# Recurrence stage: rows turned by DMA transposes, three projections in float16 halves, some waits moved

## What is computed

```python
# bounded product (L0_ffn)
out = jnp.einsum('bln,nk->blk', x, weight) * scale
v_norm = jnp.maximum(jnp.linalg.norm(out, axis=-1, keepdims=True), EPS)
out = out * (jnp.tanh(v_norm) / (v_norm + EPS))
out = out * jnp.minimum(MAX_NORM_RATIO / jnp.maximum(norm(out), EPS), 1.0)
# recurrence (L1_attn)
y = jax.nn.gelu(jnp.einsum('btd,dl->btl', x, w_y) + b_y, approximate=False)
xb = jnp.einsum('btd,dl->btl', x, w_x) + b_x
conv = conv_b + sum(conv_w[k] * xp[:, k:k + Tn] for k in range(4))   # xp: xb, padded
gate_x = jax.nn.sigmoid(jnp.einsum('btl,lm->btm', conv, w_ig) + b_ig)
gate_a = jax.nn.sigmoid(jnp.einsum('btl,lm->btm', conv, w_ag) + b_ag)
a = jnp.exp(-8.0 * gate_a * jax.nn.softplus(a_param))
h = a * h + gate_x * conv * jnp.sqrt(1.0 - a * a)                      # over the tokens
out = jnp.einsum('btl,ld->btd', h * y, w_out) + b_out
```

## Time and profile before

| what | us |
|---|---|
| median of 3 runs (1032.4 to 1034.07) | 1033.49 |
| the profiled execution | 1033.6 |
| its span, first to last instruction | 1031.9 |
| PE busy | 999.0 (97%) |
| DVE busy | 810.9 (79%) |
| ACT busy | 648.2 (63%) |
| step 2 of the recurrence, by its window | 36 |

### The profile page before, as it was taken

How to read it: one execution, slowest core, us unless ns; L and a number is a source line. 1 busy time by engine, 2 the same in 40 slices (tenths; PEclk the granted TensorE clock), 3 DMA queues, 4 the chain that set the end, 5 groups by cost and what they waited for, 6 DMA issues and landing times. The chain is left out here.

```text
span 1031.9 us, 19678 instructions
## 1 busy us (share of the span) xinstructions
PE 999.0 (97%) x7402; PEld 832.3 (81%) x7402; DVE 810.9 (79%) x1429; ACT 648.2 (63%) x1339; POOL 335.0 (32%) x456
## 2 busy tenths in 40 slices
PE   6899999999999999999999999989999999999997
PEld 6789898999989887999999989975445875875873
DVE  5998999999999998876867776885858766766763
ACT  7968786867777685665566566666232761762750
POOL 2004334152414134425344443513421331331331
PEclk9999999999999999999999999999999999999999
DMA  7520313214040454501001102023601201101101
GB/s 231 205 99 33 131 63 99 104 58 149 13 156 6 139 173 166 215 1 42 19 27 42 43 1 84 32 101 102 225 1 63 61 2 63 62 2 51 32 1 62
DMA packets 44703, 81.38 MB, mean 79 GB/s; under 512 B 7360, under 2 KB 17600, under 8 KB 42560
## 3 DMA queue, kind: packets, MB, share of 16 engines
q1 hardware_dynamic: 44608, 80.11, 22.6%
HBM read 67.24 MB, written 12.85 MB: 78 GB/s over the span
## 5 line engine op out<-in xcount | busy, mean ns | idle before, releaser
L2311 PE MATMUL banks<-d_wd,d_hh 128*128 128x512 f16 x256 | 98.1, 383 | 2.1 <-DVE d_wd L2038 2.1
L2311 PE MATMUL banks<-d_wd,d_hl 128*128 128x512 f16 x256 | 98.0, 383 | 0.0
L650 DVE SCALAR_TENSOR_TENSOR a_xs<-a_xpre,a_cvec,a_xs 128x256 f32<-128x256 f32 x192 | 91.2, 543 | 0.4 <-ACT a_xs L453 0.4
L1887 POOL TENSOR_TENSOR d_hl<-d_h32s,d_hh 128x512 f16<-128x512 f32 x48 | 55.7, 1160 | 97.4 <-ACT d_hh L1982 97.4
L822 PE MATMUL banks<-a_xth,a_wgh 128*128 128x256 f32 x256 | 74.3, 290 | 1.7 <-DVE a_wgl L592 1.7
L675 DVE TENSOR_TENSOR_SCAN a_L<-a_L,a_ident 128x512 f32<-128x512 f32 x64 | 74.8, 1212 | 0.5
L822 PE MATMUL banks<-a_xth,a_wxh 128*128 128x256 f32 x256 | 74.6, 291 | 0.0
L822 PE MATMUL banks<-a_xtl,a_wxh 128*128 128x256 f32 x256 | 72.5, 283 | 0.0
L822 PE MATMUL banks<-a_xth,a_wxl 128*128 128x256 f32 x256 | 72.4, 283 | 0.0
L822 PE MATMUL banks<-a_xtl,a_wgh 128*128 128x256 f32 x256 | 72.2, 282 | 0.0
L822 PE MATMUL banks<-a_xth,a_wgl 128*128 128x256 f32 x256 | 72.2, 282 | 0.0
(11 more groups left out here) (361 smaller groups left out, 3338.9 us busy)
## 6 DMA issues: line engine op xcount, KB each, us to landing
a_L<-decays SPq DMA_DIRECT2D x16, 1024.0 KB, 4.8
a_xf<-in_x_turned SPq DMA_DIRECT2D x16, 256.0 KB, 3.8
a_xr<-in_x SPq DMA_DIRECT2D x16, 256.0 KB, 2.7
tokens<-a_xr SPq DMA_DIRECT2D x16, 256.0 KB, 2.0
c_xb<-tokens SPq DMA_DIRECT2D x16, 256.0 KB, 2.7
d_xin<-tokens SPq DMA_DIRECT2D x16, 256.0 KB, 4.2
d_r<-tokens SPq DMA_DIRECT2D x16, 256.0 KB, 2.7
d_wd_codes<-in_down_w SPq DMA_DIRECT2D x4, 1024.0 KB, 9.3
```

The costliest lines, as they stand in the source:

```text
L650: ins = dve.scalar_tensor_tensor(out=out, in0=xpre[:, m, k:k + T], scalar=cvec[:, m, k:k + 1], in1=out, op0=ALU.mult, op1=ALU.add)
L1887: pool.tensor_tensor(hl[:, m, :], (h32s[:, m % 4, :] if i else h32[:, m % 2, :]), hh[:, m, :], ALU.subtract).then_inc(s_hl, 1)
L2311: ins = pe.matmul(ps_o[:, c % 2, :], h[:, m, cols(c)], wd[:, m, :], start=(m == 0 and h is hh), stop=(m == M - 1 and h is hl), skip_group_ ...
```

## The change

1. **Float16 halves.** Bounded, x and y use float16 instead of float32r: rows times 1024 (`X_TOP`), each weight times a factor from its norm. The factor comes from sums of squares: those of the bounded weight are built in mixer steps 1 to 5 from four small loads (`wpart`) that SP issues, with a wait for the square of the one before; those of w_x and w_y by two big ACT squares in the mixer's last step (`weight_squares`). Five small products on PE (`weight_sum`), a clip on DVE and three POOL operations (`weight_scale`) make the factors of it. The inverse factors go into the scale of the gelu, of the x projection's copy, and into c_scl (`scale_in`).
2. **Rows of steps 2 to 7.** PE's `turn_in` stays for rows 0 and 1. For the others ACT writes the high half of the untransposed rows (`rows_h`), DVE the low half (`rows_l`), and SP issues eight DMA transposes for each half (`turn_rows`, sixteen a step, 128x128 float16), for which PE's `bounded` waits.
3. **Waits moved.** In step 0 PE waits for the mixer's mean squares after the first half of the x projection and after `turn_in(1)`. `output(6)` is split in two as `output(7)` was. DVE takes `scaled(s+1)` ahead of `low_hy(s-1)`; in step 6 two of four conversions go behind `squared`. In the feed-forward stage `product` goes ahead of two conversions, and `down(0, 0)` waits for d_wd pair by pair.

The diff, cut to its core:

```diff
@@ mamba2, sync @@
+                if s <= KD:
+                    sp.wait_ge(s_wsq, 64 + 17 * (s - 1))
+                    sp.dma_start(wpart, pieces[NW][0][:, s - 1, :]).then_inc(s_wsq, 16)
                 store(s - 1)
@@ mamba2, scalar @@
+            if n is None and m is not None:
+                act.wait_ge(s_norms, 3 if i == NW else 6)
+                act.activation(hi, staged(i), ACT.Copy, scale=m).then_inc(s_whi, 1)
...
+        def weight_squares(i):
+            act.wait_ge(s_stage[i % 4], 16 * (i // 4 + 1))
+            n = KD + i - NW - 1
+            act.activation(pieces[i][1], staged(i), ACT.Square, scale=1.0 / W_TOP, accum_out=wsq[:, n:n + 1]).then_inc(s_wsq, 1)
...
             else:
-                high_piece(NW + 1)
+                weight_squares(NW + 1)
+                weight_squares(NW + 2)
+                following_stage["scale_in"]()
             own_heads(C * s + 1)
...
             high_y(C * s)
+            if 2 <= s < KD + 2:
+                part_squares(s - 2)
...
         following_stage["softplus"](1)
+        high_piece(NW + 1)
         high_piece(NW + 2)
@@ bounded_rg_lru, tiles @@
-    xth = sb_early("c_xth", [P, KD, T], F32R)
+    xth = sb_early("c_xth", [P, KD, T], F16)
...
+    sb_rows = Sbuf(nc, room["raw_y"], room["raw_y"] + 8 * KD * T)
+    rows_h, rows_l = sb_rows("c_rowsh", [P, C, D], F16), sb_rows("c_rowsl", [P, C, D], F16)
...
+    def turned(s):
+        return 2 * C + max(0, s - 1) * 2 * C * KD * 16
@@ bounded_rg_lru, sync @@
+        def turn_rows(s):
+            for src, dst, made in ((rows_h, bxh, s_bh), (rows_l, bxl, s_bl)):
+                for j in range(C):
+                    sp.wait_ge(made, C * s + j + 1)
+                    for k in range(KD):
+                        sp.dma_start(dst[:, k, cols(j)], src[:, j, k * P:(k + 1) * P], transpose=True).then_inc(s_bt, 16)
...
             for s in range(NS - 2):
+                turn_rows(s + 2)
                 if s + SLOTS < NS:
@@ bounded_rg_lru, scalar @@
             for j in range(C):
+                if s >= 2:
+                    act.wait_ge(s_x[s % SLOTS][j], 16 * (s // SLOTS + 1))
+                    act.wait_ge(s_bt, turned(s - 1))
+                    act.activation(rows_h[:, j, :], slot(s)[:, j, :], ACT.Copy, scale=X_TOP).then_inc(s_bh, 1)
+                    continue
                 act.wait_ge(s_bt, C * s + j + 1)
-                act.activation(bxh[:, :, cols(j)], ps_t[:, j], ACT.Copy).then_inc(s_bh, 1)
+                act.activation(bxh[:, :, cols(j)], ps_t[:, j], ACT.Copy, scale=X_TOP).then_inc(s_bh, 1)
@@ bounded_rg_lru, vector @@
                 dve.wait_ge(s_bh, C * s + j + 1)
+                if s >= 2:
+                    dve.wait_ge(s_x[s % SLOTS][j], 16 * (s // SLOTS + 1))
+                    dve.scalar_tensor_tensor(out=rows_l[:, j, :], in0=slot(s)[:, j, :], scalar=X_TOP, in1=rows_h[:, j, :], op0=ALU.mult, op1=ALU.subtract).then_inc(s_bl, 1)
+                    continue
...
                     recur(s - 1)
+                    if s + 1 < NS:
+                        scaled(s + 1)
                     low_hy(s - 1)
...
-                    for i in range(4):
+                    for i in range(2):
                         following_stage["convert"](i)
@@ bounded_rg_lru, tensor @@
-                pe.wait_ge(s_bl, C * s + j + 1)
+                if s < 2:
+                    pe.wait_ge(s_bl, C * s + j + 1)
+                else:
+                    pe.wait_ge(s_bt, turned(s))
...
-            if s + 1 == NS:
+            if s + 2 >= NS:
                 pe.wait_ge(s_hyh, s + 1)
...
+        def after_sums(then):
+            then(1)
+            pe.wait_ge(*last["mean_sq"])
...
-                if s + 2 < NS:
-                    turn_in(s + 2)
@@ gated_ffn @@
                 if c == 0:
                     pe.wait_ge(s_hl, M * i + m + 1)
+                    if i == 0 and m % 2 == 0:
+                        pe.wait_ge(s_prep_down, m // 2 + 1)
...
-                    pe.wait_ge(s_prep_down, len(pieces) - M)
                     down(i, 0)
```

More of the change, by code:

```diff
@@ L21 @@
 EARLY = 7
+X_TOP = 1024.0
+W_TOP = 2.0 ** 14
+W_TINY = 1e-30
 class Sbuf:
@@ L210, in mamba2 @@
     NX, NG, NW = 5, 9, len(pieces)
-    for raw, src, hi, lo in following:
-        pieces.append((src, hi, lo, None, None))
+    for raw, src, hi, lo, of_weight in following:
+        pieces.append((src, hi, lo, None, of_weight))
     def staged(i):
@@ L588, in low_piece @@
         def low_piece(i):
-            _, hi, lo, _, m = pieces[i]
+            _, hi, lo, n, m = pieces[i]
             dve.wait_ge(s_whi, i + 1)
-            if m is None:
+            if n is None and m is not None:
+                dve.scalar_tensor_tensor(out=lo, in0=staged(i), scalar=m, in1=hi, op0=ALU.mult, op1=ALU.subtract).then_inc(s_wlo, 1)
+            elif m is None:
                 dve.tensor_tensor(lo, staged(i), hi.bitcast(F32), ALU.subtract).then_inc(s_wlo, 1)
@@ L887, in sum_sq, with weight_sum @@
             last.then_inc(s_sp, 1)
+            if n == C * (KD + 2) - 2:
+                weight_sum(True, slice(0, 1))
+        def weight_sum(first, own):
+            pe.wait_ge(s_wsq, squared - (2 if first else 0))
+            if not first:
+                pe.wait_ge(s_norms, 3)
+            for k in range(KD if first else 1):
+                src = wsq[:, k:k + 1] if first else wsq[:, KD:KD + 2]
+                last = pe.matmul(ps_n[not first], ones.broadcast_to([P, P]), src, start=k == 0, stop=k == KD - 1 or not first)
+            last.then_inc(s_norms, 1)
         def x_proj(s, p):
@@ L1018, in mamba2 @@
             "gate": (s_gate, 4 * NS), "output": (s_op, C * NS), "low_output": (s_yl, C * (NS - 1)),
-            "again": {**again, "small": Again(s_small, 64), "late": Again(s_L[0], 16 * NS), "down": Again(s_L[1], 16 * NS),
+            "again": {**again, "small": Again(s_small, squared), "late": Again(s_L[0], 16 * NS), "down": Again(s_L[1], 16 * NS),
                       "x": [Again(s_stage[i], 16 * len(range(i, len(pieces), 4))) for i in range(4)],
@@ L1508, in main @@
                 squared(s)
+                if s == NS - 2:
+                    for i in range(2, 4):
+                        following_stage["convert"](i)
                 if s == 1:
@@ L2179, in main @@
                 for m in range(early, M if i == 0 else 0):
+                    for op, j in {9: ((0, 0),), 11: ((1, 0), (0, 2)), 13: ((1, 2),), 14: ((0, 4),)}.get(m, ()):
+                        weight_sums(op, j)
+                    product(i, m)
                     if 7 <= m < 10:
@@ L2182, in main @@
                         convert(2 * m - 3)
-                    for op, j in {9: ((0, 0),), 11: ((1, 0), (0, 2)), 13: ((1, 2),), 14: ((0, 4),)}.get(m, ()):
-                        weight_sums(op, j)
-                    product(i, m)
                     if m >= 12:
```

89 lines of the change are left out of this document (64 added, 25 removed).

## The result

| | before | after |
|---|---|---|
| median, us | 1033.04 | 1151.72 (1150.71 to 1152.64) |
| ratio | | 1.1148, 95% interval 1.1128 to 1.1167 |
| span of the profiled execution, us | 1031.9 | 1149.8 |
| PE busy, us | 999.0 | 998.7 |
| longest group of waits on PE in the recurrence, us | 2.9 | 124.3 |

The change makes the kernel 118.7 us slower. The forecast was 1084.3 with a range of 1044 to 1150: the direction was right, the size was not, and the time lies 1.7 us above the range's upper end.

The account below looks back on a forecast made before the run. The prediction took PE, busy 97% of the span, to bound the kernel. From 1033.6 us it took off 18.9 (12.2 + 7.4 - 0.7) and added 69.6 for six steps' transpose waits and clock loss: 1084.3 us, range 1044 to 1150.

Parts of the forecast that it names:

- What bounds the kernel: Recurrence: PE, busy 97% of the span, bounds it; only less PE work or a PE wait moves the time.
- Less work on PE: Recurrence: float16 x and y 5.9 us, bounded 2.3, dropped transposes 4.7, less 0.7 in step 7: 12.2 us gained.
- Moved waits: Step 0, step 7 and feed-forward: PE waits and clock losses removed, together 7.4 us gained.
- (a): Step 0 of the recurrence: PE's wait for the mean squares (a_rs) goes, 1.5 us gained, bounds 0.5 and 3.2.
- (b): Step 7: with two conversions moved behind, the recurrence starts earlier and PE gains 1.1 us (0 to 2.9).
- (c): Feed-forward: waits for d_h (1.0) and d_wd (2.1) and clock loss (1.7) go, 4.8 us gained (3.1 to 4.8).
- Scaling and the mixer: Five small PE products cost about 0.7 us; SP's added waits in the mixer stay hidden, 3.6 us to spare.
- Rival C: Mixer: SP's wait isn't hidden and adds 4 us, 1088 us; counted inside the forecast's 0.70.
- The transposes: Steps 1 to 6, ahead of bounded: sixteen at 0.50 us each on SP's queue, PE waits 9.0 us a step.
- Clock behind the wait: Steps 1 to 6, after PE's wait: products at half pace lose 2.6 us a step (0 to 2.9).
- Rival A: SP's queue: transposes cost about 1.4 us each, one after the other, 1164 us; chance 0.17.
- The signs: Expected: bounded's wait 50 to 60 us in all, clock about 0.5 behind, step about 46 us, SP issues 0.5 us apart.

Follow-up runs that it names:

- e10: Kernel before with one line moved: DVE scales c_ob of step s+1 ahead of c_hyl; 1028.73 us, ratio 0.9954.
- e11: Kernel before with float16 halves and their scaling, no moved waits, all rows turned by PE; 1035.14 us, ratio 1.0015.
- e2: Kernel before with all the moved waits and nothing else of the change; 1022.19 us, ratio 0.9890.
- e3: Kernel before with only the feed-forward part of the moved waits; 1030.02 us, ratio 0.9962.
- e8: Changed kernel with one 128x512 DMA transpose per half row in place of four of 128x128, 4 a step; 1059.4 us.
- e6: Changed kernel with its DMA transposes replaced by plain copies of the same 128x128 blocks, rows left unturned; 1093.7 us.
- e7: Changed kernel with only the eight high-half transposes a step, the low half's left out; 1090.5 us.
- e5: Changed kernel with transposes issued a step earlier, raw rows loaded a second time ahead of the codes, halves made in ACT's and DVE's gaps; 1016.16 us.

## Why the prediction was wrong in size, step by step

- **What bounds the kernel.** "Only two things move the time: less work on PE, or a wait on PE." That was too simple: PE at 97% hid halts of 0.2 us, behind which DVE's chain was as binding as PE's work (e10, e11).
- **Less work on PE, 12.2 us.** As a piece of this change it came about: without wait and clock a step is 56.9 - 20.7 - 2.2 = 34.0 us, 2.1 less than before, 12.9 in six. But of these I had named 1.82, and float16's 1.03 of that would have been worth nothing (e11) had not c_ob been moved.
- **Moved waits, 7.4 us.** (a) Step 0: taken 1.5, brought 1.1 in e2 and little in the changed kernel. There 0.9 us are gained from the mixer's last output products to step 1's x projection (45.2 to 44.4), and 1.8 of less work on PE are in it. The wait for a_rs is gone, and PE waits 2.6 us for c_cvh behind the y projection: DVE's convolution is next, and the clock falls there. I had not asked what is late next in step 0. (b) Step 7: the wait for c_hyl went from 2.9 to 0.4 (now for c_hyh), and 1.6 us came back as a wait for c_cvh; 2.1 us gained with x and y in float16, 1.8 summed. The number came out, its reason did not: c_ob's move alone gives 2.4 there (e10), and the 1.1 was taken for the conversions. (c) Feed-forward: 5.5 us in the trace, 4.8 taken; alone, in e3, 3.9 by the medians (2.5 to 5.3) and 4.7 by the traces from step 7 on. The move of c_ob, which my sum doesn't have at all, is worth 4.8 (e10).
- **Scaling and the mixer.** No wait of PE for it in the list. SP's broadcasts a_L that were issued at 201.88 came at 216.23, about 3 us later than I worked out, and PE was busy for all of 202 to 250 all the same. Rival C is out: PE starts the mixer's last output products at 403.35, which is within the scatter of 401.70 to 403.96. The 0.7 us for the five products no run shows by itself.
- **What was gained in all.** 124.3 of wait and 13.3 of clock make 137.6; the spans differ by 117.9; so 19.7 us were gained, 18.9 summed. That the sum is right is luck: its misses offset each other (c_ob's move left out, c_cvh's wait in step 0 left out).
- **The transposes: the step that failed.** The chain was read rightly: the first transpose starts as ACT's half is done, the x projection stands ahead, all sixteen follow one another, and PE goes on as the last one lands (452.34 + 15 x 1.27 + 2.4 = 473.8). The term that was mis-sized is "I take 0.50, the row that is nearest in count and size": it measured 1.27, the landing 2.4 for 2.2. That is 15 x 0.77 = 11.6 us of the 11.7 by which the wait exceeded the 9.0 taken. Six times that is 70 us; the forecast missed by 67.4.
- **Clock behind the wait.** 2.6 taken, 2.2 measured (1.5 to 2.9). It hardly depends on the length of the wait: 1.3 to 2.9 behind waits from 5.6 to 21.3 us, with means of 1.8 (e8), 2.1 (e6), 2.2 (e7) and 2.2 (after).
- **Rival A** (about 1.4 us each, 1164 us) was the mechanism, with 1.27 in place of 1.39. Its chance of 0.17 was too low; the range had taken in its nearer half and ends just under the time. The bounds of 0.303 and 1.389 came from transfers that transposed nothing; a sum over sixteen of them in a chain stands or falls with that one number, and nothing in the trace spoke for the middle of it.
- **The signs.** The new first entry in PE's waits, the clock at 0.5 behind it, an x projection of 5.2 us and bounded at 0.216 a product where the clock is full, and no wait for d_wd: all seen. The 50 to 60 us of wait and the step of 46 us were not (124 and 56.9). "If the spacing on SP isn't near 0.5 us, the price of a transpose is" what failed: it is.

## What to carry to other kernels

A price that no row of the trace shows, times sixteen in a row on one queue, decides by itself: forecast both ends as cases, and don't settle on the nearest row because it is near. A DMA transpose was paid for by the instruction on its queue, 128x512 like 128x128, so make each as wide as it can be, and start it where something long stands between it and its reader; the same transposes cost 131 us more than PE's in the chain, and at most 1 us a step earlier. Before a bound engine's work is made shorter, measure the distance of starts at each hand-over: halts of 0.2 us stood in no list of waits here, and showed that a second chain was as long as the first.

## What the runs showed of the hardware

- A DMA transpose in float16 from SBUF to SBUF holds SP's queue for 1.23 us (128x128) or 1.27 us (128x512) and lands 2.4 or 2.5 us after its issue in the median (at most 5.2); a plain copy of 128x128 0.60 and 1.8 (e6, e8).
- PE's clock behind a pause: the loss was 1.3 to 2.9 us behind each of 24 pauses of 5.6 to 21.3 us (after, e6, e7, e8), with hardly a trend by length.
- DVE's c_rowsl took 0.69 us or 1.75 us for the same 128x512 in the changed kernel. The tile view, POOL's timeline of that time in the changed kernel, and DVE's in e5, where POOL is idle:

```profile
L1444 DVE SCALAR_TENSOR_TENSOR c_rowsl<-c_xb,c_rowsh x12: 691/1222/1754, 452.3 to 737.0; 128x512 f16<-128x512 f32 x12
```

```profile
507.34 2.96 POOL L1272 TENSOR_TENSOR c_xb<-c_xb,c_bo 128x512 f32<-128x512 f32 x2
```

```profile
516.76 1.29 DVE L1465 SCALAR_TENSOR_TENSOR c_rowsl<-c_rowsraw,c_rowsh 128x512 f16<-128x512 f32 x2 [0.73 <-ACT c_rowsh L1338]
```

In the changed kernel each of the six pairs takes 2.36 us and starts beside POOL's addition of the bias; in e5 the four pairs with POOL idle take 1.29, and the one beside POOL's work, in step 0, 3.45. Before, c_bxl, another operation, which reads the banks, had taken 1.29 for two at the same place. That the two engines get in each other's way there is what the rows suggest; no run tested it by itself.
